# Another head and tail for an adaLN attention and mixture kernel: scales by rows, half projections, modulation ahead of the input's transposes

## What is computed

```python
mod = (silu(c) @ wmod).reshape(4, 6, 1, 256)      # sa, ca, ga, sb, cb, gb; c is 4x256, wmod 256x1536
h = layernorm(x) * (1 + ca) + sa
q, k, v = (h @ (codes * repeat(scales, 32, axis=0)) + b for each)   # 256 -> 16 heads x 128
attn = softmax(q @ k.T / sqrt(128)); o = attn @ v
x = x + ga * (o @ wo + bo)                        # |ga| >= 0.25
h = layernorm(x) * (1 + cb) + sb
x = x + gb * (h @ W.T + top-2-of-8 LoRA experts of rank 16, by a softmax router)
```

## Time and profile before

| what | value |
|---|---|
| median of 3 runs | 777.44 us (777.26 to 777.73) |
| the profiled execution: time, span | 777.42 us, 775.5 us |
| busy: PE, PEld, DVE, ACT, POOL | 99%, 86%, 83%, 67%, 62% of the span |
| the chain that ended last | PE 95% of the span |
| instructions | 14722 |

### The profile page before, as it was taken

How to read it: one execution, slowest core, us unless ns; L and a number is a source line. 1 busy time by engine, 2 the same in 40 slices (tenths; PEclk the granted TensorE clock), 3 DMA queues, 4 the chain that set the end, 5 groups by cost and what they waited for, 6 DMA issues and landing times.

```text
span 775.5 us, 14722 instructions
## 1 busy us (share of the span) xinstructions
PE 766.5 (99%) x4206; PEld 667.7 (86%) x4206; DVE 647.5 (83%) x1254; ACT 517.6 (67%) x1124; POOL 483.4 (62%) x454
## 2 busy tenths in 40 slices
PE   7999999999999999999999999999999999999998
PEld 6888888888888888888888888888888888888887
DVE  5889888888888888888888888888898888879876
ACT  2788676667666676667666766676667676766841
POOL 4686576548655675556657575655667476789722
PEclk9999999999999999999999999999999999999999
DMA  7554355444454335444445434543355334433202
GB/s 216 162 154 124 95 147 150 139 107 99 118 144 131 95 96 139 129 124 98 110 133 147 98 94 122 146 125 95 96 145 152 95 94 107 112 89 86 56 1 109
DMA packets 71898, 90.67 MB, mean 117 GB/s; under 512 B 19574, under 2 KB 37431, under 8 KB 71867
## 3 DMA queue, kind: packets, MB, share of 16 engines
q1 hardware_dynamic: 53184, 74.00, 37.3%
q10 hardware_dynamic: 18682, 16.30, 7.0%
HBM read 22.06 MB, written 2.11 MB: 31 GB/s over the span
## 4 chain that ended last, share of the span: by engine, by line
PE 95%; POOL 1%; DVE 1%; DMA 1%; ACT 1%; SPq 1%; issue 0%; DVEq 0%
PE score L1102 9%; PE score L1103 9%; PE score L1104 9%; PE qv L1102 8%; PE qv L1103 8%; PE qv L1104 8%; PE o L1102 7%; PE o L1104 7%; PE o L1103 7%; PE ky L1102 4%; PE ky L1103 4%; PE ky L1104 4%; PE y L1102 2%; PE y L1104 2%; PE y L1103 2%; DMA stage<-in_L_attn_wk_scales_dram 1%
## 5 line engine op out<-in xcount | busy, mean ns | idle before, releaser
L404 POOL TENSOR_TENSOR pT_lo<-pT,pT_hi 128x512 fp32r<-128x512 f32 x248 | 314.6, 1305 | 240.7 <-ACT pT_hi L576 240.6
L660 ACT ACTIVATE prob<-score,neg_max 128x512 f32<-128x512 f32 x256 | 172.7, 688 | 79.7 <-DVE neg_max L941 79.5
L941 DVE TENSOR_REDUCE neg_max<-score 128x1 f32<-128x512 f32 x256 | 159.7, 682 | 1.6 <-PE score L1104 1.6
L954 DVE STREAM_TRANSPOSE pB<-prob 128x512 f32<-128x512 f32 x252 | 156.4, 678 | 0.0
L576 ACT ACTIVATE pT_hi<-pT 128x512 fp32r<-128x512 f32 x248 | 135.3, 620 | 0.0
L1102 PE MATMUL score<-k_hi,q_hi 128*128 128x512 f32 x256 | 101.2, 395 | 0.6 <-DVE k_lo L862 0.6
L1103 PE MATMUL score<-k_lo,q_hi 128*128 128x512 f32 x256 | 100.3, 392 | 0.0
L1104 PE MATMUL score<-k_hi,q_lo 128*128 128x512 f32 x256 | 99.7, 389 | 0.0
L1102 PE MATMUL o<-pT_hi,v_hi 128*128 128x512 f32 x248 | 96.6, 389 | 0.0
L1104 PE MATMUL o<-pT_hi,v_lo 128*128 128x512 f32 x248 | 96.5, 389 | 0.0
L1103 PE MATMUL o<-pT_lo,v_hi 128*128 128x512 f32 x248 | 96.5, 389 | 0.0
(11 more groups left out here) (262 smaller groups left out, 1824.7 us busy)
## 6 DMA issues: line engine op xcount, KB each, us to landing
pT<-pB SPq DMA_DIRECT2D x1008, 64.0 KB, 2.0
out_dram<-x_nat SPq DMA_DIRECT2D x8, 256.0 KB, 2.1
stage<-in_L_attn_wv_codes_dram ACTq DMA_DIRECT2D x7, 256.0 KB
stage<-in_L_attn_wv_scales_dram ACTq DMA_DIRECT2D x14, 128.0 KB
stage<-in_L_attn_wq_codes_dram ACTq DMA_DIRECT2D x7, 256.0 KB
stage<-in_L_attn_wq_scales_dram ACTq DMA_DIRECT2D x14, 128.0 KB
stage<-in_L_attn_wk_codes_dram ACTq DMA_DIRECT2D x7, 256.0 KB
stage<-in_L_attn_wk_scales_dram ACTq DMA_DIRECT2D x14, 128.0 KB
```

Of the source, the lines that this page charges most:

```text
L404: pool.tensor_tensor(split(pT_lo, kt), turned(par, kt), split(pT_hi, kt).bitcast(f32), ALU.subtract).then_inc(p_lo_ok, 1)
L660: act.activation(prob[:, i], score_ps[i][:, :], ACT.Exp, bias=neg_max[:, i:i + 1], accum_out=row_sum[:, s % 2, i:i + 1]).then_inc(exp_ok, 1)
L941: dve.tensor_reduce(neg_max[:, i:i + 1], score_ps[i][:, :], AX.X, ALU.max, negate=True).then_inc(max_ok, 1)
L954: dve.transpose(pB[:, s % 2, :, i].rearrange("p g k q -> p k g q"), prob[:, i].rearrange("p (k g q) -> p k g q", k=QT, g=G)).then_inc(pB_o ...
```

## The change

Head. The scales of q, k and v come as four rows each, by one transfer on ScalarE's queue into memory that VectorE zeroed, and TensorE spreads them over the partitions with a 0/1 matrix (`spread_rows`). The first part of wmod comes in four transfers. All three first products are VectorE's (`first_product`). TensorE does the modulation in two halves with fillers between them, ahead of the transposes of z; of z's four tiles one is made by ScalarE. k comes before q, and both are projected, biased and split in halves of 256 tokens in banks of their own; the first two score tiles wait only for q's first half. The statistics of batch 1 stand among this work, batch 1's z is VectorE's and is made in step 0; the order of VectorE's work in steps 0 and 1 is new.

Tail. In the last step ScalarE makes batch 0's input before v's high part, VectorE takes the maxima before v's low part; the rows of batch 0 go to y's bank; y_add of step N - 3 is split and stands between the low parts of the last probabilities; `ffn_input` waits for its banks one by one; TensorE's order of dense, ffn_input and lora_rows is changed, and ScalarE's of weighted_lora_out(1) and odds(1).

The diff's core (indentation reduced):

```diff
+def load_rows(queue, m):
+    src = bass.AP(SCALES[m].tensor, 0, [[FEAT, NB], [NB * FEAT, 2], [1, PW]])
+    queue.wait_ge(rows_zero, 1 + "kqv".index(m))
+    queue.dma_start(scale_rows[m][0:NB], src).then_inc(ld_rows[m], 16)
+def first_scales(m):
+    return {"q": o_ps[0], "k": o_ps[1], "v": score_ps[0]}[m][:, :].rearrange("p (c n) -> p c n", c=2)
+mod_banks = (ky_ps, qv_ps)
+half_banks = dict(q=(qv_ps, o_ps[0]), k=(ky_ps, o_ps[1]))
+def half_tokens(u):
+    return slice(u * S // 2, (u + 1) * S // 2)
...
-sp.dma_start(wmod_1, mod_cols[:, :, 0:GA * P]).then_inc(ld_wmod, 16)
+for c in range(DC):
+    for t in (SA, CA):
+        cols = slice((t + c) * P, (t + c + 1) * P)
+        sp.dma_start(wmod_1[:, :, cols], mod_cols[:, :, cols]).then_inc(ld_wmod_c[c], 16)
 def load_x(b):
     sp.dma_start(x_nat[:, b * QT:(b + 1) * QT], x[b].rearrange("(p t) d -> p t d", p=P)).then_inc(ld_x[b], 16)
+load_first(sp, "k")
 load_first(sp, "q")
-load_first(sp, "k")
 load_x(1)
 load_first(sp, "v")
 load_x(2)
...
 inverse_std(0)
+parts("k", 0, 0)
 parts("q", 0, 0)
-product("k", 0)
-parts("k", 0, 0)
+parts("v", 0, 0)
 parts("q", 0, 1)
 inverse_std(1)
-product("v", 0)
-parts("v", 0, 0)
 parts("k", 0, 1)
...
+load_rows(act, "k")
+load_rows(act, "q")
+act.wait_ge(c_tr, 1)
+act.activation(c_exp[:, :], qv_ps[:, 0:B * DC], ACT.Exp, scale=-1.0).then_inc(c_exped, 1)
+load_rows(act, "v")
 for i, vec in enumerate((bq, bk, bv)):
     act.dma_start(vec_raw[i * NH:(i + 1) * NH, :], vec.rearrange("(h p) -> h p", p=P)).then_inc(ld_vec, 16)
 act.wait_ge(bv_zero, 1)
 act.dma_start(bv_wo[0:1], bo.rearrange("(o d) -> o d", o=1)).then_inc(ld_bo, 16)
-act.wait_ge(c_tr, 1)
-act.activation(c_exp[:, :], o_ps[0][:, 0:B * DC], ACT.Exp, scale=-1.0).then_inc(c_exped, 1)
 def scale_codes(p):
     act.wait_ge(ld_w["q"], LDW * p)
     act.wait_ge(w_prod["q"], p)
     act.activation(codes["q"][:, :, :], codes["q"][:, :, :], ACT.Copy, scale=SCORE_SCALE).then_inc(wq_scaled, 1)
-act.wait_ge(mod_mm, 1)
-act.activation(modT[:, SA:SA + DC], ky_ps[:, 0:DC * B].rearrange("p (j b) -> p j b", b=B), ACT.Copy).then_inc(mod_ok, 1)
-act.activation(modT[:, CA:CA + DC], ky_ps[:, DC * B:2 * DC * B].rearrange("p (j b) -> p j b", b=B), ACT.Copy,
-               bias=1.0).then_inc(mod_ok, 1)
-act.wait_ge(mod_ok, 2)
+def modulation_out(c):
+    act.wait_ge(mod_mm, c + 1)
+    act.activation(modT[:, SA + c], mod_banks[c][:, 0:B], ACT.Copy).then_inc(mod_ok, 1)
+    act.activation(modT[:, CA + c], mod_banks[c][:, B:2 * B], ACT.Copy, bias=1.0).then_inc(mod_ok, 1)
+    act.wait_ge(mod_ok, 2 * (c + 1))
 def input_high(b, c, bank):
...
+act.activation(z[:, 0, QT - 1], x_nat[:, QT - 1], ACT.Identity, bias=shift[:, 0, QT - 1:QT],
+               scale=rstd[:, 0, QT - 1:QT]).then_inc(z_act_ok, 1)
+for c in range(DC):
+    modulation_out(c)
 for c in range(DC):
     input_high(0, c, score_ps[2 + c])
+act.wait_ge(h_ev, 2)
+act.activation(hT_hi[:, 1, tokens(0)], hT32[:, 1], ACT.Copy).then_inc(h0_hi, 1)
+act.wait_ge(vec_tr, 1)
+act.activation(vecT[:, NH:VECS], score_ps[1][:, NH:VECS], ACT.Copy).then_inc(vec_ok, 1)
+act.activation(vecT[:, 0:NH], score_ps[1][:, 0:NH], ACT.Copy, scale=SCORE_SCALE).then_inc(vec_ok, 1)
 act.wait_ge(vec_ok, 2)
 act.activation(bias_now[:, 0:2], bias[:, 0:2, 0:2], ACT.Copy).then_inc(bias_ok, 1)
 act.wait_ge(bias_ok, 1)
...
+def half_high(m, u):
+    act.wait_ge((half_mm[m], {"q": q_mm, "k": k_mm}[m])[u], 1)
+    act.activation({"q": q_hi, "k": k_hi}[m][:, half_tokens(u)], half_banks[m][u][:, 0:S // 2], ACT.Identity,
+                   bias=bias_now[:, "qk".index(m), 0:1]).then_inc((half_hi[m], {"q": q_hi_ok, "k": k_hi_ok}[m])[u], 1)
+for m in "kq":
+    for u in range(2):
+        half_high(m, u)
...
+if end:
+    ffn_input_out(0, 0, o_ps[0])
+    ffn_input_out(0, 1, ky_ps)
 if not start:
     v_out(n + 1, batch_of(s) % 2, s % 2)
...
-if end:
-    ffn_input_out(0, 0, o_ps[0])
-    ffn_input_out(0, 1, ky_ps)
...
+weighted_lora_out(1)
 odds(1)
-for b in range(1, B):
+for b in range(2, B):
     weighted_lora_out(b)
...
+for m in "kqv":
+    dve.memset(scale_rows[m], 0.0).then_inc(rows_zero, 1)
+dve.memset(block_rows, 0.0).then_inc(block_zero, 1)
+dve.wait_ge(ident_ok, 1)
+dve.wait_ge(block_zero, 1)
+dve.tensor_copy(block_rows[0:NB], ident[0:NB, 0:NB].unsqueeze(2).to_broadcast([NB, NB, BLK])).then_inc(block_ok, 1)
 dve.wait_ge(c_exped, 1)
...
-normalise(0)
-dve.wait_ge(ld_w_first["q"], LDW_FIRST)
-dve.scalar_tensor_tensor(out=w32["q"][:, :, :], in0=codes["q"][:, :, :], scalar=SCORE_SCALE, in1=scales["q"][:, :, :],
-                         op0=ALU.mult, op1=ALU.mult).then_inc(w_prod["q"], 1)
-for c in range(DC):
-    input_hi(0, c)
-    input_lo(0, c)
-dve.wait_ge(vec_tr, 1)
-dve.tensor_copy(vecT[:, NH:VECS], o_ps[1][:, NH:VECS]).then_inc(vec_ok, 1)
-dve.tensor_scalar(vecT[:, 0:NH], o_ps[1][:, 0:NH], SCORE_SCALE, None, ALU.mult).then_inc(vec_ok, 1)
+dve.wait_ge(ln_rstd, 1)
+dve.scalar_tensor_tensor(out=shift[:, 0], in0=mv[:, 0, :, 0], scalar=-1.0, in1=rstd[:, 0], op0=ALU.mult,
+                         op1=ALU.mult).then_inc(shift0_ok, 1)
+normalise(0, range(QT - 1))
+def first_product(m):
+    dve.wait_ge(ld_w_first[m], 16)
+    dve.wait_ge(rows_mm[m], 1)
+    dve.scalar_tensor_tensor(out=w32[m][:, :, :], in0=codes[m][:, :, :], scalar=SCORE_SCALE if m == "q" else 1.0,
+                             in1=first_scales(m), op0=ALU.mult, op1=ALU.mult).then_inc(w_prod[m], 1)
+first_product("k")
+first_product("q")
+input_hi(0, 0)
+input_lo(0, 0)
+dve.wait_ge(ld_x[1], 16)
+row_statistics(1, 0)
+row_statistics(1, 1)
+input_lo(0, 1)
+first_product("v")
+row_statistics(1, 2)
+row_statistics(1, 3)
 dve.wait_ge(vec_ok, 2)
...
+half_low("k", 1)
+half_low("q", 0)
+half_low("q", 1)
+variances(1)
 def head_slice(p, s):
...
-if not start:
+if not start and not end:
     v_low(n + 1, batch_of(s) % 2, s % 2)
 maximum(0)
 maximum(1)
 maximum(2)
 maximum(3)
 if end:
+    v_low(n + 1, batch_of(s) % 2, s % 2)
+    statistics(1)
     inverse()
-    statistics(1)
     o_low(n - 1)
     prob_low(n - 1, (s - 1) % 2, range(QT))
+elif start:
+    normalise(1, range(2))
+    v_low(1, 0, 0, ky_ps)
+    normalise(1, range(2, QT))
+    q_low(n + 2, head_slice(p, s + 1))
+    turn(0)
+    k_low(n + 2, head_slice(p, s + 1))
+    input_hi(1, 0)
+    turn(1)
+    input_hi(1, 1)
+    turn(2)
+    turn(3)
+    inverse()
+elif first and s == 1:
+    dve.wait_ge(ld_x[2], 16)
+    statistics(2)
+    turn(0)
+    turn(1)
+    q_low(n + 2, head_slice(p, s + 1))
+    turn(2)
+    k_low(n + 2, head_slice(p, s + 1))
+    turn(3)
+    inverse()
 else:
     turn(0)
     turn(1)
-    if start:
-        v_low(1, 0, 0, ky_ps)
     turn(2)
     turn(3)
     inverse()
-    if start:
-        dve.wait_ge(ld_x[2], 16)
-        row_statistics(2, 0)
     if not early:
...
-    end_low(kt)
+y_add(N - 3, B - 2, 1, False, tiles=range(2))
+end_low(0)
+end_low(1)
+y_add(N - 3, B - 2, 1, False, tiles=range(2, QT))
+end_low(2)
+end_low(3)
 o_low(N - 1, ky_ps)
 y_add(N - 2, B - 1, 2, False)
...
 pe.wait_ge(ident_ok, 1)
+keep_busy(4, score_ps[0])
 pe.wait_ge(ld_c, 16)
-pe.transpose(o_ps[0][:, 0:B * DC], c_raw[:, :], ident[0:B * DC, 0:B * DC]).then_inc(c_tr, 1)
-for i in range(20):
-    pe.transpose(score_ps[0][:, (i % QT) * P:(i % QT + 1) * P], ident[:, :], ident[:, :])
-pe.wait_ge(ld_wmod, 16)
+pe.transpose(qv_ps[:, 0:B * DC], c_raw[:, :], ident[0:B * DC, 0:B * DC]).then_inc(c_tr, 1)
+keep_busy(6, score_ps[0])
+def spread_rows(m):
+    pe.wait_ge(block_ok, 1)
+    pe.wait_ge(ld_rows[m], 16)
+    for c in range(2):
+        ins = pe.matmul(first_scales(m)[:, c], block_rows[:, :, :].rearrange("a b q -> a (b q)"), scale_rows[m][:, c],
+                        start=True, stop=True)
+    ins.then_inc(rows_mm[m], 1)
+spread_rows("k")
+spread_rows("q")
+keep_busy(4, score_ps[0])
 pe.wait_ge(silu_ok, 1)
 silu = c_silu[:, :].rearrange("p (b c) -> p c b", c=DC)
-for j in range(SA, GA):
-    for c in range(DC):
-        ins = pe.matmul(ky_ps[:, j * B:(j + 1) * B], wmod_1[:, c, j * P:(j + 1) * P], silu[:, c],
-                        start=(c == 0), stop=(c == DC - 1))
-ins.then_inc(mod_mm, 1)
+for u in range(DC):
+    pe.wait_ge(ld_wmod_c[u], 16 * 2)
+    for i, j in enumerate((SA + u, CA + u)):
+        for c in range(DC):
+            ins = pe.matmul(mod_banks[u][:, i * B:(i + 1) * B], wmod_1[:, c, j * P:(j + 1) * P], silu[:, c],
+                            start=(c == 0), stop=(c == DC - 1))
+    ins.then_inc(mod_mm, 1)
+    keep_busy(4, score_ps[0])
+for u in range(DC):
+    for t in range(QT):
+        if t < QT - 1:
+            pe.wait_ge(z_ok, t + 1)
+        else:
+            pe.wait_ge(z_act_ok, 1)
+        ins = pe.transpose(INPUT_BANKS[0][u][:, t * P:(t + 1) * P], z[:, 0, t, u * P:(u + 1) * P], ident[:, :])
+    ins.then_inc(h_tr, 1)
 def transpose_input(b):
-    if b == 0:
-        pe.wait_ge(z_ok, QT)
+    if b == 1:
+        pe.wait_ge(z_ok, QT * 2 - 1)
     else:
-        pe.wait_ge(zin_ok, QT * b)
+        pe.wait_ge(zin_ok, QT * (b - 1))
```

(60 more changed lines are left out.)

98 lines of the change are left out of this document (54 added, 44 removed).

## The result

| | before | after |
|---|---|---|
| median, runs (lowest to highest) | 777.53, 12 runs (777.16 to 778.07) | 779.77, 12 runs (778.25 to 781.13) |
| the profiled execution: time, span | 777.42, 775.5 | 780.23, 778.4 |
| first score matmul (F) | 20.43 | 17.97 |
| last transpose of head 0's probabilities ends | 27.88 | 30.71 |
| head 0's weighted sum ends (q of the next step starts) | 47.45 | 50.38 |

The ratio after to before is 1.0029, with a 95% interval of 1.0022 to 1.0037: slower, and more than the 0.2% that this measurement can tell. The range of the prediction ended at 779.3. The spread differs too: in these twelve runs each, before holds within 0.9 us and after spreads over 2.9.

The account below looks back on a forecast made before the run. TensorE, without idle time between 60 and 700 us, was taken to bound the kernel, so only the ends could give. Head +0.3 and tail -0.65 made 777.42 + 0.3 - 0.65 = 777.1, range 775.5 to 779.3.

Parts of the forecast that it names:

- What bounds the kernel, and where the gain of F goes: Head: TensorE bounds the middle; F's gain of 2.2 to 3.8 is mostly lost before head 0's weighted sum.
- Steps 1 to 4: Head up to the first score: scales by rows, earlier modulation, one z tile on ScalarE; F = 16.6 or 18.2.
- the second case: Head: half clock until 7.4, z's transposes at 10.9, F = 18.2, 1.1 lost.
- the first case: Head: full clock from the first spread on, z's transposes at 9.4, F = 16.6, 0.5 gained.
- The rival of a late half clock: Head: half clock lasts through the modulation ahead of z, F = 20.0, time 779.7; chance 0.19.
- Step 5: VectorE's new order after the first scores: last transpose at F + 12.0, head 0's weighted sum ends at F + 30.4.
- This chain of 18.4 doesn't get shorter by the change: Head 0, last transpose through 16 SyncE copies and low parts to the weighted sum's end: 18.4, as before.
- Waits added in between cost nothing more: TensorE before head 0's weighted sum: new waits, about 1 before project_v, cost 0, covered by the 16 copies.
- C: Follow-up theory: head 0's 16 copies and GpSimd's low parts set the head's end; e3 lands them 1.9 earlier, 777.9.
- the prediction's own formula: Whole kernel: 777.42, less the head's gain of 17.1 - F, less the tail's 0.65.
- Step 6: Tail: gaps of 0.30 and 0.62 go, one of 0.28 comes; sum -0.65, between -0.2 and -1.3.
- signs of being wrong: Head 0: transposes ending before F + 11, chain behind them shorter than 18.4, or F outside 16.1 to 19.3.

Follow-up runs that it names:

- e2: The changed kernel with 12 filler transposes in front of project_v's wait in step 1, the wait itself kept; 780.13.
- e3: The changed kernel with three of head 0's 16 copies issued by ScalarE instead of SyncE; 779.42.
- e8: The changed kernel with the three copies on ScalarE of e3 and the 12 fillers of e2; 777.93.
- e4: The changed kernel with VectorE's order of step 0 as before, the four transposes and v_low ahead of batch 1's z; 778.11.
- e1: The changed kernel with VectorE's q_low in step 1 put between batch 2's row statistics and its variances; 779.54.
- e11: e9 with two of batch 1's four z tiles on ScalarE, and step 1's q_low put behind two transposes and two row statistics; 779.81.
- e12: e11 with 18 filler transposes in the idle time; 776.87.
- e6: e4 with 12 filler transposes before project_v's wait in step 1, as in e2; 777.48.
- e5: The changed kernel with the q order of e1, 4 fillers before project_v of step 1 and the three copies on ScalarE of e3; 781.3.
- e9: e4 with step 1's fourth transpose of probabilities ahead of k_low; 776.46.
- e7: The kernel before with the tail's part of the change alone; 777.17 beside 777.51.

## Why the prediction was wrong

*What bounds the kernel, and where the gain of F goes: right.* The first scores came 2.5 earlier and nothing of it was left at the weighted sum, whose end went from 47.45 to 50.38; e2, e3 and e8 showed both paths to it.

*Steps 1 to 4, right, both cases of them.* In the profile a spread pass took 0.45 (5.89 - 4.11 for four), the full clock came only near 7.6, z's transposes were at 10.62 and F at 17.97: the second case (10.9, 18.2). The record of the granted clock reads 1.00 there all the same; the length of the passes shows what it doesn't. In e2's execution the same code had the full clock at 5.4, z's transposes at 9.30 and F at 16.91: the first case (9.4, 16.6). In the twelve profiles with this head F lies at 16.91 once and at 17.58 to 18.28 otherwise, so the forecast's middle (17.4) was 0.5 to 0.9 too early for ten of them. The rival of a late half clock (F = 20) didn't come, though its time of 779.7 did, by another way. The memset of 512 columns took 0.48, against the 0.6 taken. The estimate of 0.53 by the Trainium skill, page "VectorE: DVE Perf Modes", section "Zero memsets can be issued as uint32 (trn2)", was the nearer one.

*Step 5, the mechanism right, its sizes short.* The last transpose came at F + 12.7 instead of F + 12.0. The timeline of VectorE has both reasons, and below them stand GpSimd's instructions of the same time:

```profile
21.62 2.00 DVE L863 SCALAR_TENSOR_TENSOR z<-x_nat,mv,rstd 128x256 f32<-128x256 f32 x2
...
24.14 0.87 DVE L863 SCALAR_TENSOR_TENSOR z<-x_nat,mv,rstd 128x256 f32<-128x256 f32 x2
...
27.41 0.43 DVE L869 CAST hT_hi<-hT 128x512 fp32r<-128x512 f32 x1
27.76 0.70 DVE L1036 STREAM_TRANSPOSE pB<-prob 128x512 f32<-128x512 f32 x1
28.39 1.11 DVE L869 CAST hT_hi<-hT 128x512 fp32r<-128x512 f32 x1
```

```profile
21.64 1.30 POOL L405 TENSOR_TENSOR stage<-stage 128x512 f32<-128x512 f32 x1
27.92 1.29 POOL L426 TENSOR_TENSOR hT_lo<-hT,hT_hi 128x512 fp32r<-128x512 f32 x1 [4.98 <-DVE hT_hi L869]
```

Two tiles of z took 2.00 beside GpSimd's product and 0.87 without it, a cast 1.11 beside GpSimd's low part and 0.43 without. The cast ends 0.29 after GpSimd's instruction (29.50 and 29.21). The two transposes of probabilities at 29.42, beside GpSimd's next low part (29.57 to 30.87), took 1.29, as in e4 at 23.70 with GpSimd idle. In e4, with transposes in that place, the long cast (1.41 there) came behind the last transpose, where no copy waits for it. By the Trainium skill, page "SBUF — State Buffer", section "SBUF: two separate sides", VectorE and GpSimd share one pair of ports as a lock: a GpSimd instruction, or one of VectorE in a fast mode or with two inputs from SBUF, whichever starts first, holds the pair for its whole length and the other waits. The trace agrees, down to the transposes, which have one input and didn't wait.

*The steps that failed.* The prediction let the sum of head 0 end at F + 30.4; it ended at F + 32.4. Two steps had no room for that, and each of them was enough.

The first is "This chain of 18.4 doesn't get shorter by the change": the size was taken as fixed, and it took 19.7 (30.71 to 50.38). Its part from the last transpose to the last landing was read off one profile as 11.7, and here it took 13.0 (43.76 - 30.71). It isn't bad luck of one run alone: in e1 and e2, whose set of copies also starts near 30 or 31, it took 12.8 and 12.3, each with one copy slow to issue (1.86 and 1.28); in the six runs whose set starts near 25 it took 11.6 to 12.0, as in the kernel before. Why the later sets are longer stays open. With the 0.7 of VectorE's list (F + 12.7 instead of F + 12.0) this makes the 2.0, and by this chain the profiled execution ended. e2 shows it with TensorE's wait gone: at full clock it still took 779.84 and 780.55.

The second is "Waits added in between cost nothing more". The waits were forecast in place and size (1.18 before project_v), and their cover, the copies, was there. What was put at nothing is TensorE's clock behind them: 6.8 us at half clock, from 38.3 to 45.2, hold 3.4 us of work, so TensorE was ready for the sum at 46.83 instead of 43.4. Had the copies kept to 18.4, the sum would have ended at 49.6 by TensorE's own path, still 1.2 behind the forecast (an estimate, from 46.83 and 12 passes 0.23 apart). e3 shows it with the copies out of the way (0.35 gained of the 1.9 that C expected), and e11 against e12 gives the size, 2.9. Only e8, with both mended, gets down to 777.93.

With the measured F of 17.97 the prediction's own formula gives 777.42 + (17.97 - 17.1) - 0.65 = 777.6. The profiled execution took 2.6 more: 0.7 and 1.3 from step 5, 0.4 from step 6, and 0.2 between that sum and 69 (2.93 behind there, 3.12 at 69).

*Step 6, mis-sized.* Of the forecast -0.65 came -0.2. As forecast: the gaps of 0.30 and 0.62 gone, the new one before ffn_input(3) 0.33 (0.28 forecast). Not forecast: the gap before the last weighted sum grew to 0.46 instead of shrinking to 0.35 (reckoned as in the prediction), and 0.3 came in two places behind 764, at lora_transpose(1) (764.88) and at the last dense (769.34) and what follows it. The term's lower end, -0.2, is what came, but the gap that it named, before lora_transpose(0), didn't: that one starts without a wait, at 763.50.

*The range* ended at 779.3 since its only large loss was a late F; a loss between the first score and the weighted sum had no place in it. Its signs of being wrong had the same blind side: they watched for a chain shorter than 18.4, and none of them came.

## What to carry to other kernels

Time gained at the start is worth only what arrives at the next join of chains; list every chain into it, and what brings each one's last instruction forward. Never count a wait on TensorE as free because something later binds: behind it the clock can be halved, here for 3 to 7 us, and then the slack on which it was free is gone. Fillers in its place help only if no other chain holds the time (e8 and e12, but not e2), and cost time if they are longer than the wait (e6). Better: order the work so that the instruction that starts the longest chain (here the transposes ahead of 16 copies) comes first. And look at pass lengths and granted clock beside the busy share, and at the clock of each single execution: the two executions at 1.000 in e2, and the two in e3, told as much as another experiment.

## What the runs showed of the hardware

- Half clock followed idle times of TensorE of 1.18 (changed kernel), 1.19 (e3), 1.69 (e11), 2.27 (e1), 2.30 (e5) and 2.46 (e2), and not those of 0.75 (e8) and 1.05 (e4, e9), in the profiled executions. Ahead of those at 37 to 38 stood tiny modulation matmuls of 4 columns. The length alone doesn't decide: 1.49 in the kernel before and 1.24 in e7, before k's first projection, left the clock at 1.00. Nor is it certain: 2 of e11's 12 executions and 2 of e3's 11 kept 1.000. The row of the kernel before, behind which the passes start 0.23 apart:

```profile
17.12 0.50 PE L1102 MATMUL ky<-hT_hi,wk_hi 128*128 128x512 f32 x1 [1.49 <-POOL wk_lo L390]
```

- When the full clock first comes differs between executions of the same code, by up to 2 us here (5.4 in e2, near 7.6 in the changed kernel), and F with it, by 1.1.
- Now and then one of SyncE's copies takes 1.1 to 2.1 to issue instead of 0.59, and the copies around it land up to 3.9 after their issue instead of 2.0. In the changed kernel this hit the last copy of head 0; in the kernel before it first came at 50.7, where it cost nothing. What sets its place wasn't tried.
